# A delta-rule layer on TensorE: the projections of a quad grouped, one activation table, a new order of all steps

## The reference

```python
kn = k_t / jnp.maximum(jnp.linalg.norm(k_t, axis=-1, keepdims=True), 1e-12)
pred = jnp.einsum('bhji,bhj->bhi', S, kn)
r = jnp.clip(v_t - pred, -CLIP, CLIP)
S = a_t[..., None] * S
kp = jnp.einsum('bhd,bhde->bhe', kn, S)
S = S + b_t[..., None, None] * kn[..., None] * (v_t - kp)[..., None, :]
o = jnp.einsum('bhji,bhj->bhi', S, q_t)
R = aR_t[..., None] * R
kpR = jnp.einsum('bhd,bhde->bhe', kn, R)
R = R + g_t[..., None, None] * kn[..., None] * (r - kpR)[..., None, :]
o = o + jnp.einsum('bhji,bhj->bhi', R, q_t)
```

## Time and profile before

| | us |
|---|---|
| median of 3 runs | 2267.28 |
| lowest, highest | 2261.83, 2269.86 |
| span of the profiled execution, first to last instruction | 2258.0 |
| TensorE busy in the span | 2181.8 (97%) |
| VectorE busy | 1765.0 (78%) |
| ScalarE busy | 1374.6 (61%) |
| GpSimd busy | 1144.9 (51%) |

### The profile page before, as it was taken

One profiled execution on the slowest core, in us unless ns is written; L12 is line 12 of the kernel. 1 busy time (PEld: TensorE's weight loads), 2 busy tenths in 40 slices (PEclk: granted clock), 3 DMA queues, 4 the chain that ended last, 5 costly groups with the idle time before them and its releaser, 6 DMA issues.

```text
span 2258.0 us, 114502 instructions
## 1 busy us (share of the span) xinstructions
PE 2181.8 (97%) x49472; PEld 1824.6 (81%) x49472; DVE 1765.0 (78%) x3791; ACT 1374.6 (61%) x2391; POOL 1144.9 (51%) x2384
## 2 busy tenths in 40 slices
PE   8999987899999999999999999999999999999997
PEld 3455545788888888888888888888888888888987
DVE  5501115699999889999999899999888989999984
ACT  3333256566666666666666666666666666666640
POOL 0010004666666566566666666656656666666641
PEclk9999998799999999999999999999999999999999
DMA  3000000222222322222222222222223232233331
GB/s 95 0 1 0 22 0 17 70 68 69 68 68 68 74 55 70 67 68 67 69 67 69 74 66 69 68 68 68 68 69 72 68 71 69 69 70 72 72 75 48
DMA packets 336179, 134.92 MB, mean 60 GB/s; under 512 B 285505, under 2 KB 324545, under 8 KB 335681
## 3 DMA queue, kind: packets, MB, share of 16 engines
q1 hardware_dynamic: 334480, 125.24, 23.5%
q10 hardware_dynamic: 1200, 2.36, 0.4%
HBM read 66.69 MB, written 60.82 MB: 56 GB/s over the span
## 4 chain that ended last, share of the span: by engine, by line
PE 94%; DMA 2%; DVE 1%; issue 1%; POOL 1%; ACT 1%; SPq 0%; POOLq 0%; DVEq 0%; ACTq 0%
PE bank L569 13%; PE bank L594 5%; PE bank L585 5%; PE bank L417 4%; PE bank L430 4%; PE bank L615 3%; PE bank L606 3%; PE bank L671 3%; PE bank L730 3%; PE bank L535 3%; PE bank L516 3%; PE bank L639 3%; PE bank L503 3%; PE bank L526 3%; PE bank L659 3%; PE bank L546 3%
## 5 line engine op out<-in xcount | busy, mean ns | idle before, releaser
L1210 POOL TENSOR_TENSOR lane_t<-lane_n,lane_x 128x15 f32<-128x15 f32 (+7 forms) x960 | 290.8, 303 | 321.5 <-DMA lane_n<-n_dram 251.3
L569 PE MATMUL bank<-kq,Kt 64*64 64x96 f32 x8192 | 363.3, 232 | 8.9 <-DVE AS L979 7.0
L1213 POOL TENSOR_TENSOR lane_x<-lane_x,lane_t 128x15 f32<-128x15 f32 (+7 forms) x960 | 305.2, 318 | 75.2
L569 PEld LDWEIGHTS bank<-kq,Kt 64*64 64x64 f32 x8192 | 316.2, 135 | 14.1 <-issue 13.6
L1167 POOL TENSOR_TENSOR dk<-cum 128x512 f32<-128x512 f32 x64 | 69.7, 1089 | 306.6 <-DVE cum L928 306.6
L1356 ACT ACT_TABLE_LOAD x128 | 164.2, 1283 | 91.7 <-PE bank L594 90.5
L1399 ACT ACTIVATE kend<-Kt,ek 128x64 f32<-128x64 f32 x768 | 189.5, 336 | 0.0
L1184 POOL TENSOR_TENSOR KQF<-efull,kn 128x768 f32<-128x768 f32 x64 | 136.3, 2130 | 84.6 <-ACT efull L1377 84.4
L928 DVE TENSOR_TENSOR_SCAN cum<-rst,dk 128x512 f32<-128x512 f32 x128 | 156.9, 1226 | 20.7 <-ACT dk L1356 20.7
L979 DVE COPY_PREDICATED AS<-cst,bank 128x384 f32<-128x384 int32 x256 | 141.3, 577 | 6.4 <-PE bank L569 6.1
L867 DVE TENSOR_TENSOR dn<-bank,s3b 128x512 f32<-128x512 f32 x8 | 5.5, 691 | 172.6 <-PE bank L442 167.6
(11 more groups left out here) (165 smaller groups left out, 6308.1 us busy)
## 6 DMA issues: line engine op xcount, KB each, us to landing
k_dram<-kend SPq DMA_DIRECT2D x64, 384.0 KB, 3.0
kend_in<-k_dram SPq DMA_DIRECT2D x256, 96.0 KB, 2.4
XF<-x_dram SPq DMA_DIRECT2D x256, 64.0 KB, 2.3
lane_n<-n_dram SPq DMA_DIRECT2D x128, 124.0 KB, 3.2
x_dram<-lane_x SPq DMA_DIRECT2D x128, 124.0 KB, 2.4
n_dram<-AS SPq DMA_DIRECT2D x256, 32.0 KB, 2.0
n_dram<-AR SPq DMA_DIRECT2D x256, 32.0 KB, 1.6
wt<-in_win SPq DMA_DIRECT2D x4, 640.0 KB, 4.2
```

The costliest lines, as they stand in the source:

```text
L569: ins = pe.matmul(v3(dst[hd[h], o:o + kinds * C], kinds)[:, :, i * SUB:(i + 1) * SUB], Kt[hd[h], m * 96 + i * SUB:m * 96 + i * SUB + C], r ...
L1210: pool.tensor_tensor(tv, lane_n[:, m * SUB + m + 1:m * SUB + BASE].unsqueeze(2).to_broadcast([L, rows, m + 1]), xv[:, m, 0:m + 1].unsqueez ...
L1213: pool.tensor_tensor(xv[:, m + 1:, 0:m + 1], xv[:, m + 1:, 0:m + 1], tv, ALU.subtract).then_inc(s["lane_step"], 1)
```

## The change

1. `project_kq` is split; `project_k`, `project_q`, `project_out` (of quad k-2), `project_a` and `project_r` stand behind each other in TensorE's body, q in PA1, a in PR0, r in PR1. Products 0 and 1 of quad k+1 now wait until the gate of S of quad k+2 is read from PR0 and v of quad k+2 from PR1.
2. v is projected into PR1 between `level1_nx` and `level1_zd`, and the norms come right behind `level1_zd`.
3. ScalarE loads one table set that has both ln and exp ahead of the loop, and again behind each late batch of gelus.
4. The clamp of the squared norms on VectorE is gone. ScalarE's ln reads the norms from PSUM with a floor of 1e-30 as bias, and `norm_k` takes the smaller of 1e12 and one over the norm in the same instruction that multiplies k.
5. The bodies of all five queues have a new order. SyncE issues `keys_in` ahead of `lanes_out`; GpSimd's `against_state` and `far_half` run a body later, `small_inverses` of quad k+1 follows them, then `far` of quad k+3.

```diff
-            def project_kq(n):
+            def project_k(n):
                 need(pe, "w_loaded", (n // B + 1) * 16)
                 need(pe, "kn", n)
-                need(pe, "vt_sb", n)
                 for p in range(2):
                     ins = pe.matmul(PA0[:, p * T:(p + 1) * T], wcol(1, p), xh(n), start=True, stop=True)
                 ins.then_inc(s["k_ps"], 1)
+
+            def project_q(n):
+                need(pe, "w_loaded", (n // B + 1) * 16)
+                need(pe, "rn_ln", n)
                 for p in range(2):
                     ins = pe.matmul(PA1[:, p * T:(p + 1) * T], wcol(0, p), xh(n), start=True, stop=True)
                 ins.then_inc(s["q_ps"], 1)
@@ -511,44 +516,47 @@
                     late_third(0)
 
             def project_a(n):
-                need(pe, "q_sb", n + 1)
+                need(pe, "w_loaded", (n // B + 1) * 16)
+                if n < 2:
+                    need(pe, "ea_sb", n)
+                else:
+                    need(pe, "pr_sb", OPS * (n - 2) + OPS - 1)
                 for p in range(2):
-                    ins = pe.matmul(PA1[:, p * T:(p + 1) * T], wcol(2, p), xh(n), start=True, stop=True)
+                    ins = pe.matmul(PR0[:, p * T:(p + 1) * T], wcol(2, p), xh(n), start=True, stop=True)
                 ins.then_inc(s["a_ps"], 1)
                 if n == 0:
                     late_second(1)
                 elif n == 1:
                     late_third(1)
 
+            def project_r(n):
+                need(pe, "w_loaded", (n // B + 1) * 16)
+                need(pe, "pr_sb", OPS * (n - 2) + OPS)
+                need(pe, "vt_sb", n)
+                for p in range(2):
+                    ins = pe.matmul(PR1[:, p * T:(p + 1) * T], wcol(3, p), xh(n), start=True, stop=True)
+                ins.then_inc(s["r_ps"], 1)
+                if n == 0:
+                    late_second(2)
+                elif n == 1:
+                    late_third(2)
+
             def norms(n):
                 need(pe, "k_sq", n + 1)
-                need(pe, "er_sb", n + 1)
+                need(pe, "q_sb", n + 1)
                 pe.matmul(PA1[:, :], cst[:, M_BD:M_BD + P], ksq[:, :], start=True, stop=True).then_inc(s["n2_ps"], 1)
                 if n == 0:
                     late_second(3)
                 elif n == 1:
                     late_third(3)
 
-            def project_r(n):
-                need(pe, "ea_sb", n + 1)
-                for p in range(2):
-                    ins = pe.matmul(PA1[:, p * T:(p + 1) * T], wcol(3, p), xh(n), start=True, stop=True)
-                ins.then_inc(s["r_ps"], 1)
-                if n == 0:
-                    late_second(2)
-                elif n == 1:
-                    late_third(2)
-
             def project_v(n):
-                need(pe, "n2_cl", n + 1)
+                need(pe, "er_sb", n + 1)
                 for c in range(NCH):
                     for h in range(2):
-                        ins = pe.matmul(PA1[hd[h], c * P:(c + 1) * P], xh(n)[:, c * C:(c + 1) * C], wt[:, 4 * 256 + h * P:4 * 256 + (h + 1) * P],
+                        ins = pe.matmul(PR1[hd[h], c * P:(c + 1) * P], xh(n)[:, c * C:(c + 1) * C], wt[:, 4 * 256 + h * P:4 * 256 + (h + 1) * P],
                                         start=True, stop=True)
                 ins.then_inc(s["v_ps"], 1)
-                if n == 1:
-                    for tb in range(4):
-                        late_last(tb)
 
...
                 need(pe, "kfar", n + 1)
-                need(pe, "pr_sb", OPS * n + g - 1)
+                if g == 0:
+                    need(pe, "ea_sb", min(n + 2, NQ))
+                elif g == 1:
+                    need(pe, "vt_sb", min(n + 2, NQ))
+                else:
...
-            def clamp_norms(n):
-                need(dve, "n2_ps", n + 1)
-                need(dve, "kn", n)
-                dve.tensor_scalar(n2[:, :], PA1[:, :], NORM_MIN2, None, ALU.max).then_inc(s["n2_cl"], 1)
-
             def norm_k(n):
                 need(dve, "rn_sb", n + 1)
                 need(dve, "kfull", n)
                 need(dve, "kfar", n)
-                dve.tensor_tensor(kn[:, :], PA0[:, :], n2[:, :], ALU.mult).then_inc(s["kn"], 1)
+                dve.scalar_tensor_tensor(out=kn[:, :], in0=n2[:, :], scalar=RN_MAX, in1=PA0[:, :], op0=ALU.min, op1=ALU.mult).then_inc(s["kn"], 1)
 
             def running_sums(n, y):
...
+            def load_ln_exp():
+                act.add_instruction(mybir.InstLoadActFuncSet(act_func_set_id=LN_EXP_SET, name=nc.get_next_instruction_name()))
...
             def norms(n):
-                need(act, "n2_cl", n + 1)
-                act.activation(n2[:, :], n2[:, :], ACT.Ln, scale=float(2 ** NORM_SHIFT)).then_inc(s["rn_ln"], 1)
+                need(act, "n2_ps", n + 1)
+                need(act, "kn", n)
+                act.activation(n2[:, :], PA1[:, :], ACT.Ln, scale=float(2 ** NORM_SHIFT), bias=small[:, 3:4]).then_inc(s["rn_ln"], 1)
                 need(act, "rn_ln", n + 1)
                 act.activation(n2[:, :], n2[:, :], ACT.Exp, scale=-0.5, bias=small[:, 1:2]).then_inc(s["rn_sb"], 1)
...
             def body(k):
                 a, b, d, e = on(k + 3), on(k + 2), on(k), on(k - 1)
-                if b:
-                    copy_v(k + 2)
-                    from_anchor(k + 2)
-                    gate_inverse(k + 2)
-                if a:
-                    copy_q(k + 3)
                 if d:
                     level0(k)
                 if a:
                     gate(k + 3, 0)
+                    copy_q(k + 3)
+                    squares(k + 3)
                     log_decay(k + 3, 0)
-                    squares(k + 3)
+                    gate(k + 3, 1)
+                    log_decay(k + 3, 1)
                 if d:
                     level1(k)
                 if a:
-                    gate(k + 3, 1)
-                    log_decay(k + 3, 1)
+                    copy_v(k + 3)
                     norms(k + 3)
+                    from_begin(k + 3)
                 if e:
                     copy_out(k - 1)
                 if b:
                     to_end(k + 2)
                 if a:
-                    from_begin(k + 3)
+                    from_anchor(k + 3)
                     to_anchor(k + 3)
-
+                    gate_inverse(k + 3)
+
+
+            load_ln_exp()
             for k in range(-3, LAST + 3):
                 body(k)
 
```

More of the change, by code:

```diff
@@ L68 @@
     "cl_s": "S's held in range", "cl_r": "R's held in range", "ls_sb": "log decays of S", "lr_sb": "log decays of R",
-    "n2_cl": "squared norms held above the floor", "rn_ln": "their logarithms", "rn_sb": "one over the norms",
+    "rn_ln": "their logarithms", "rn_sb": "one over the norms",
     "kn": "normed k", "cum": "running sums of log decays within a chunk (2)", "dm": "sums from the anchors",
@@ L571, in products @@
                 ins.then_inc(s["pr_ps"], 1)
+                if n == 0 and g == 3:
+                    for tb in range(4):
+                        late_last(tb)
             def level0_nx(n):
@@ L734, in body @@
             def body(k):
-                a, b, l, d, e, f = on(k + 3), on(k + 2), on(k + 1), on(k), on(k - 1), on(k - 2)
+                a, b, l, e, f = on(k + 3), on(k + 2), on(k + 1), on(k - 1), on(k - 2)
                 if f:
-                    r_s(k - 2, 2)
-                    s_p(k - 2, 3)
+                    s_s(k - 2, 2)
+                    r_s(k - 2, 1)
                 if e:
-                    level1_zd(k - 1)
+                    level0_nx(k - 1)
                 if f:
-                    s_o(k - 2, 3)
+                    s_o(k - 2, 2)
+                    s_p(k - 2, 2)
+                if e:
+                    level0_zd(k - 1)
+                if f:
+                    s_w(k - 2, 3)
+                    r_o(k - 2, 1)
+                    r_w(k - 2, 2)
+                    s_y(k - 2, 3)
                 if l:
```

206 lines of the change are left out of this document (101 added, 105 removed).

## The result

The changed kernel takes 2301.68 us (median of 4 runs, 2298.89 to 2302.89), the kernel before 2268.57 in the same series (4 runs, 2261.83 to 2278.46): a ratio of 1.0132, interval 1.0097 to 1.0167. It is slower; 2187 was predicted. The profiled execution's span is 2298.4 us, against 2258.0: 40.4 more, where the medians differ by 33.1.

The account below looks back on a forecast made before the run. TensorE was taken as the bound, 94% of the chain. 61 x (1.30 - 0.15) = 70, with 3 and 7 a gain of 80 us on 2258.0: 2178, plus 9.3 to the median, 2187; range 2160 to 2230.

Parts of the forecast that it names:

- Tile shapes: TensorE's switches between tile shapes: their cost falls from 2.24 to 0.94 us a body, saving 1.30, bounds 0.90 and 1.35.
- rival A: TensorE's exits from level 1 and v cost 0.15 each, so 0.90 is saved, not 1.30; 2212 us, chance 0.13.
- Table loads: On ScalarE, four loads of 1.28 us a body go, off the path before and after, so worth 0.
- rival C: ScalarE's table loads stay, three between level 0's and level 1's copies; 54 us slower, 2321; chance 0.05.
- The clamp and VectorE's room: VectorE loses 0.69 us a body, leaving 25.4 busy of 27.1 and 1.7 of room; no gain in itself.
- Queues: GpSimd's `small_inverses` ends by 15 us into a body, its result wanted 12 later; SyncE's `keys_in` moves ahead; cost 0.
- Weights: Next four heads' weights load behind v, 12 us left instead of 3; gain of 3 us, bounds 0 and 6.7.
- Hand-offs: Results reaching TensorE slightly late in the new order cost 0.15 us a body, bounds 0 and 0.5.
- First bodies: Second projection of k no longer waits behind the decays' exps for `copy_v`; gain of 7 us, bounds 0 and 15.
- The end: The last body's chain is as long as before, so 0.
- Rival B: VectorE's hand-offs become the bound, TensorE loses 0.9 us a body; 2233, chance 0.15; no gain left from 1.46.
- The range: Whole kernel's time: the forecast case's own range 2163 to 2205 us; with A and nearly B, 2160 to 2230.

Follow-up runs that it names:

- the kernel with all three costs taken away: Changed kernel with weights' load ahead of `lanes_out`, GpSimd's large steps cut to a few columns, small inverses shortened (output not the reference's): 2197.07 us against 2265.94, ratio 0.9702.

## Why the prediction was wrong, step by step

- **Tile shapes, 1.30 us a body: right.** The rows asked for of the projections, v, the norms and level 1 came as forecast, and rival A (exits that cost 0.15) is out. The shortest body did not: 27.88 for 27.1 to 27.3, above the 27.7 that was to show the forecast wrong.
- **Table loads, and rival C: right.** There is none in the loop, and the kernel with this part alone is no slower. The rule of the Trainium skill in "ScalarE: Activation LUTs", "Table sets: the hidden batching unit", that one set holds exp and ln, is borne out here.
- **The clamp and VectorE's room: failed.** The prediction said VectorE would be left with "25.4 busy of 27.1". This holds for the old order (25.3 in the kernel with one table and no clamp). In the new order VectorE was busy for 27.3 on average, since its steps fell beside other GpSimd steps. I took the durations of the earlier trace rows as properties of the steps; they belong to a pair of queues.
- **Queues, "0": failed.** `small_inverses` was given 11 us and 12 in hand. But its result has two transfers and two runs of issues around it; the whole was 27.0 us and became 31.4, and it was never written down as a chain. Of the 12 us in hand some 8 are taken by the way back through DRAM. In the changed kernel TensorE waits 21.2 us for it; once the weights were early, shortening it gave 18 to 32 us.
- **Weights, a gain of 3: wrong in sign.** I had noted that SyncE issues the load "behind `lanes_out`", and gave it a bound of 0 at the low side. It waits there for GpSimd. It cost 24 to 30 us: 14.9 in waits, 8.3 by the lower clock behind them. The three failed terms (VectorE's room, the chain, the weights) are of like size, and none alone explains the miss.
- **Hand-offs, 0.15: not the loss that was feared, but something is missing.** In the kernel with all three costs taken away the waits named by VectorE and ScalarE in the loop are few, and the shortest full body is 27.1. But its mean is 28.05 for 27.74. The prediction left the stalls put down to "issue" as they are; they rose from 7.9 us to 27.1 there, and to 32.5 in the changed kernel. Why is open.
- **First bodies, a gain of 7: right in number** (6.7), and by luck: a wait of 8.1 us for XF that nobody forecast lies there, and the kernel without the three costs gains 19.5. **The end, 0: wrong**; 13.2 us are lost behind quad 63, with 6.1 of waiting for XF and a granted clock of 0.86.
- **Rival B** had the engine right (VectorE late) and the cause wrong: not that many thin hand-offs fail, but that steps become longer. Its limit of 1.46 us a body was passed: 27.74 became 29.45, 1.71 more, of which the bodies with new weights are 0.37.
- **The range.** Its working gives no source for the 2205. The bounds stated, 0.90 saved and 0.5 lost a body, give 61 x 0.40 = 24 us, which is 2243. That is still far below what was measured.

## What to carry over

A body in balance has as many constraints as queues: before moving steps, write down for each queue what then runs beside it, and follow each chain that leaves the core's engines (through DRAM and back) from end to end with its issues in series. A duration read beside one neighbour does not hold beside another: VectorE's steps with two SBUF inputs, and GpSimd's, are to be laid side by side in the new order and the overlap charged in full to the second, and long GpSimd steps were better in halves here. A load that stands behind a wait on an in-order queue is as late as that wait, so the rarely issued ones (weights) go first.

## Not expected of the hardware

- A stall of TensorE can cost more than its length: 24 to 30 us came back for 15 us of waits, with a granted clock of 0.74 to 0.75 over 20 us and matmuls of 256 columns at twice their time. Once a clock of 0.69 followed 1.35 us of standing; that the one caused the other is not shown.
- GpSimd and VectorE exclude each other by whole instructions even in plain fp32 work: 2.52 us for a step of 1.22.
- Issues in series are a cost of their own: 0.45 to 0.50 us each on SyncE in these rows; taking 5 of the chain's 16 to another queue was worth 18 to 26 us in 64 bodies.
